# Two products with the state in a chunked delta-rule kernel: matmuls issued with the two batches alternating

## The reference, cut to what matters

```python
def step(Sst, inp):
    qt, kt, vt, gt, bt = inp
    Sst = Sst * jnp.exp(gt)[..., :, None]
    err = vt - jnp.einsum('bhk,bhkv->bhv', kt, Sst)
    Sst = Sst + bt[..., None, None] * kt[..., :, None] * err[..., None, :]
    ot = jnp.einsum('bhk,bhkv->bhv', qt, Sst)
    return (Sst, ot)
```

## Time and profile before

| | us |
|---|---|
| median of three runs | 1710.4 |
| lowest, highest | 1701.67, 1733.17 |
| profiled execution, first to last instruction | 1705.8 |
| PE busy, DVE busy in it | 1461.6, 1112.7 |
| mean granted TensorE clock in it | 0.919 of full |

### The profile page before, as it was taken

The page is one execution under the profiler, slowest core; times in us unless marked ns, Lnnn a source line. Parts: engine busy times, 40 slices in busy tenths (PEclk is TensorE's granted clock), DMA queues, the critical chain, the costliest instruction groups (busy, mean ns, idle before and its releaser), DMA issues.

```text
span 1705.8 us, 25673 instructions
## 1 busy us (share of the span) xinstructions
PE 1461.6 (86%) x9434; PEld 1185.9 (70%) x9434; DVE 1112.7 (65%) x2013; ACT 560.4 (33%) x1082; POOL 392.1 (23%) x351
## 2 busy tenths in 40 slices
PE   5786899999878699999978699999978599999977
PEld 4432788888733588888833488888853378888866
DVE  4399576667469567667549756766729856666742
ACT  1286222222268322122148422212228522222221
POOL 5034022212124112112124211221214311211210
PEclk8798899899999799899989799989989789999986
DMA  4000100000000010000000010000000000000001
GB/s 107 1 0 1 50 1 1 0 0 0 1 14 1 3 48 1 0 0 0 1 14 1 0 50 1 0 0 0 0 15 0 1 1 1 1 0 0 0 1 25
DMA packets 12493, 14.59 MB, mean 9 GB/s; under 512 B 3124, under 2 KB 8310, under 8 KB 12406
## 3 DMA queue, kind: packets, MB, share of 16 engines
q1 hardware_dynamic: 12406, 13.48, 2.7%
HBM read 12.43 MB, written 1.05 MB: 8 GB/s over the span
## 4 chain that ended last, share of the span: by engine, by line
PE 52%; DVE 25%; issue 19%; ACT 2%; POOL 1%; SPq 1%; DVEq 1%; POOLq 0%; DMA 0%; ACTq 0%
PE bank L653 9%; PE bank L707 8%; PE bank L703 8%; PE bank L690 5%; DVE qkv L950 4%; DVE ks L983 4%; PE bank L821 4%; DVE kq L981 3%; DVE tot L984 2%; PE bank L667 2%; PE bank L723 2%; PE bank L659 2%; PE bank L714 2%; DVE nmat L989 2%; DVE aq L990 2%
## 5 line engine op out<-in xcount | busy, mean ns | idle before, releaser
L653 PE MATMUL bank<-kq,ks 128*128 128x128 f32 x1536 | 231.6, 296 | 53.1 <-DVE tot L984 47.2
L981 DVE TENSOR_TENSOR kq<-kq,tot 128x512 f32<-128x512 f32 x160 | 138.4, 865 | 194.5 <-PE bank L653 191.4
L653 PEld LDWEIGHTS bank<-kq,ks 128*128 128x128 f32 x1536 | 200.9, 202 | 69.2 <-DVE tot L984 59.9
L629 PE MATMUL bank<-hT,gw 128*128 128x512 f32 x384 | 185.7, 621 | 38.1 <-DVE region L957 19.1
L950 DVE SCALAR_TENSOR_TENSOR qkv<-region,gchan,qkv 128x512 f32<-128x512 f32 x192 | 201.1, 1099 | 0.0
L371 POOL TENSOR_TENSOR qkv<-qkv,kq 128x509 f32<-128x509 f32 (+2 forms) x96 | 133.2, 1388 | 282.9 <-ACT qkv L454 277.9
L690 PE MATMUL bank<-region,nmat 128*128 128x64 f32 x1280 | 173.4, 280 | 2.3
L707 PE MATMUL bank<-tt,fmat 128*128 128x64 f32 x1280 | 170.6, 277 | 5.5 <-DVE fmat L1019 5.5
L629 PEld LDWEIGHTS bank<-hT,gw 128*128 128x128 f32 x384 | 73.6, 198 | 142.7 <-issue 103.7
L690 PEld LDWEIGHTS bank<-region,nmat 128*128 128x128 f32 x1280 | 163.6, 199 | 12.4 <-DVE nmat L989 7.5
L707 PEld LDWEIGHTS bank<-tt,fmat 128*128 128x128 f32 x1280 | 160.6, 195 | 7.5 <-DVE fmat L1019 6.0
(11 more groups left out here) (156 smaller groups left out, 2419.6 us busy)
## 6 DMA issues: line engine op xcount, KB each, us to landing
gw<-in_L_attn_Wq SPq DMA_DIRECT2D x4, 512.0 KB, 4.0
gw<-in_L_attn_Wk SPq DMA_DIRECT2D x4, 512.0 KB, 5.0
gw<-in_L_attn_Wv SPq DMA_DIRECT2D x4, 512.0 KB, 6.0
gwo<-in_L_attn_Wo SPq DMA_DIRECT2D x4, 512.0 KB, 4.9
x<-in_L_attn_hidden_states SPq DMA_DIRECT2D x2, 512.0 KB, 6.1
gfb<-in_L_attn_Wfb SPq DMA_DIRECT2D x4, 256.0 KB, 6.2
ggb<-in_L_attn_Wgb SPq DMA_DIRECT2D x4, 256.0 KB, 7.3
out<-x SPq DMA_DIRECT2D x2, 512.0 KB, 5.5
```

The source lines that it names most:

```text
L629: last = eng.matmul(bank[t][:, :], gw[:, t, kt, cols], hT[:, kt, toks], start=(kt == 0), stop=(kt == KT - 1))
L653: last = eng.matmul(o[:, :, u, :].rearrange("p a (n t) -> p a n t", t=h), unit(ks[:, p], u), half(kq[:, p, :, u * P:(u + 1) * P], h, 1), s ...
L981: eng.tensor_tensor(half(kq[:, p], h, 1), half(kq[:, p], h, 1), lower.rearrange("p (a n o) -> p a n o", a=1, o=1).broadcast_to((P, 2, nb, ...
```

## The change

Both pairs of loops are turned inside out. Each matmul, its operands, its output and its flags are what they were; only their order within the 8 is another: head 0 of batch 0, head 0 of batch 1, head 1 of batch 0, and so on. The wait ahead of the 8 stays ahead of them and the signal behind them stays with the last.

```diff
                     eng.wait_ge(state_ready, B * m + g + 1)
-                    for b in range(B):
-                        for u in range(G):
+                    for u in range(G):
+                        for b in range(B):
                             last = eng.matmul(unit(bank[4], u)[b * C:(b + 1) * C, :],
                                               kq[:, q, 0, u * P + b * C:u * P + (b + 1) * C],
                                               unit(state[:, b], u), start=True, stop=True)
...
-                    for b in range(B):
-                        for u in range(G):
+                    for u in range(G):
+                        for b in range(B):
                             eng.matmul(unit(bank[5], u)[b * C:(b + 1) * C, :],
                                        kq[:, q, 1, u * P + b * C:u * P + (b + 1) * C],
                                        unit(state[:, b], u), start=(u == 0), stop=False, skip_group_check=True)
```

## The result

The changed kernel takes 1811.97 us (median of 4 runs, 1805.08 to 1818.16), the old one 1709.87 (1701.67 to 1733.17). The ratio is 1.0616, 95% interval 1.0576 to 1.0656: 6% slower. Not one run of either kernel lies in the other's spread. Medians here are of all runs; ratios leave out runs over 1.5% above their kernel's fastest.

What follows compares the result with a forecast made beforehand. TensorE was 52% of the chain, VectorE 25%, with VectorE setting the pace in middle slots. First scan slots -1.2 and last slots -2.0 gave -3.2 us on the 1705.8 span: 1702.6, a median of 1707 us, range 1692 to 1727.

Steps and rivals of the forecast that it cites:

- what the order does to a product: Either product at full clock: alternating batches overlap throughout, so it takes 1.145 us instead of 1.58, 0.435 us less.
- The sum over L730: Sign in the profile after: L730's PE busy time falls from 55.8 to about 40 us.
- the middle slots: First product in 24 middle slots: gain 0, because VectorE sets the pace; L653 and L1031 start as before.
- the last slots: Last slot of each of 4 groups, both products: -0.5 us each, -2.0 us, as L753 comes 1.97 us after the start.
- the first scan slot: First product in 4 first scan slots, at 1.2 GHz: -0.3 us each, between 0 and 0.33, -1.2 us in all.
- 0 for the second product in the 28 slots: Second product in middle and first scan slots: gain 0, since PE then waits for VectorE's decays of level 1.
- the clock falls more often: Rival: thinner work behind the second product drops TensorE's clock; one more slow slot per group, +16.4 us, 1727; chance 0.13.
- a gap of 1.7 into one of 2.1: Behind the second product, ahead of level 2's product: the gain only lengthens PE's gap, in us.
- that the halves do not overlap: Rival: a product takes as long as before or 2.0 us, +3.6 us in all, 1710 to 1714; chance 0.06.

Runs made afterwards that it cites:

- e6: Changed kernel (both products alternating) plus 2 extra half-width matmuls behind the second product, both in the same output half: 1716.88 us, ratio 1.0052.
- e1: Old kernel with only the first product (L730) alternating, the second in its old order: 1709.22 us, ratio 1.0048.
- e4: Changed kernel plus 6 extra matmuls streaming 1 column each, in the gap behind the second product: 1806.34 us, ratio 1.059.
- e7: Changed kernel plus 2 extra half-width matmuls behind the second product, one in each output half, running at once: 1810.85 us, ratio 1.0566.
- e9: Old kernel, old orders, no filler; L667 streams 128 columns of ones instead of 1, L659 uses 128 rows instead of 16: 1694.85 us, ratio 0.9927.

## Why the prediction was wrong

The prediction chose next to no change, 1707 us, with a range of 1692 to 1727. Measured 1812.

**Right: what the order does to a product.** Forecast 1.145 us, measured 1.09 at full clock: the second half starts with the first, not 0.055 us behind it. The sum over L730 was forecast at 40 us and is 36.7; three of the four products in first scan slots ran partly at full clock (1.31 to 1.44 us, not 2.03).

**Right: the middle slots.** L653 and L1031 start where they did, and the gap grew by 0.49 (forecast 0.4). That alternation gives and costs nothing there at full clock is shown by e6 (34.26 us).

**Right: the last slots.** 2.50 became 1.97, as the sum of 1.97 had it, 2.1 us for the four. It is lost in the rest.

**Wrong in size: the first scan slot.** The term was -0.3 for each; e1 shows 0, the lower end of its bound. Not only the stretched tail of L984 but L981 as well ran into POOL's L343.

**The step that failed: 0 for the second product in the 28 slots, with the clock left to a rival, "the clock falls more often".** The rival's place was right, the gap behind the second product; its size was taken as "one more such slot in each group", 16.4 us net, and its chance as 0.13. In fact 19 of the 24 middle slots have that fall instead of 4, all 24 have some fall instead of 8, and together they take 80.4 us more. The first scan slots, which the rival left out, take 29.1 more. The old slots of 34.26 us have the same gap and keep their clock, and I read that as "it hangs on something that the change may tip" and then priced a small tip.

The price had a misreading too. The fall of the earlier trace rows stands in the slot from 318.10, which took 35.47 us, 1.2 more than 34.26. The slot of 39.20 in the earlier trace rows, from which the 4.9 us were taken, has its falls 23.3 and 30.2 us in, at other places. That 16 more slots at 4.9 us come to 78, near the 80.4, is luck.

Beyond that, two things were missed.

First, I counted what the change takes from this place as idle time, "a gap of 1.7 into one of 2.1". But e4 shows that idle time does not decide it here, and e6 and e7 that streaming in two halves at once did less for the clock than the same streaming in a row. Before, only the middle of a product had the two batches side by side. After, all of it does. The forecast named exactly this as the gain: "two batches share the array without taking time from one another". It is the loss as well.

Second, the falls are not independent. A slot with a fall is longer, so the next slot meets the clock's changes at another place. In the old kernel this leads back to slots without a fall: 16 of 24 have none. In the new one not one of the 24 is free of a fall. That is counted; that the place behind the second product catches the slots that used to get through is my reading of it, and the rule by which the chip decides was not measured.

**Rightly held unlikely: that the halves do not overlap (0.06).** The rule of the Trainium skill, "TensorE: Matmul & The Clock Gate", section "The mechanism" of Part 3, that weight loads overlap matmuls only when row groups differ, would have meant this, and it is contradicted again: 16 instructions with all rows and different output columns start in pairs. The Trainium skill's "TensorEngine Tiling (Array Packing)", section "Key Properties", says that different tiles can load weights and multiply in parallel. The trace agrees with that: two begin within 0.04 us.

What stays open is the rule behind the clock. The counts say only which of these kernels kept it and which did not.

## What to carry to other kernels

Before shortening TensorE work that nobody waits for, ask what it does for the clock: here a saving of 0.49 us in a place with slack brought slots of up to 43.6 us instead of 34.3 to 34.5. Packing two small products into the array at once shortens them truly, but in a stretch in which TensorE has little to stream it can cost more than it gives, and the busy time of the stretch does not show it; compare the granted clock slot by slot. In a kernel of many equal slots curing one thin place can move the fall to the next, so look at all slots after a change, and try the cheapest thickening first (more columns or rows in an instruction that is there anyway, as in e9).

## What the runs showed of the hardware

- Two matmul streams with the same rows and different halves of the output columns start within 0.04 us of one another, and each keeps its own pace of 0.11 us. In the old order, where the second batch begins while the first runs, they alternate at 0.054 (in rows of the last slot).
- 12 instructions that stream 1 column, busy for 1.50 us in the profile, left the falls of the clock as they were (22 of 24 slots); 12 that stream 128, busy for 1.60 us, removed them (0 of 24).
- The same 4 instructions behind the second product left the clock's falls at 5 of 24 slots when one followed the other (e6) and at 21 of 24 when two and two ran at once (e7).
- The product with 16 rows takes a little longer than with 128. In the old kernel, from its start to the next product's start:

```profile
270.13 1.15 PE L659 MATMUL bank<-beta,gsel 16*128 x8
...
271.21 1.10 PE L703 MATMUL bank<-fmat,tt 128*128 128x64 f32 x8
```

that is 1.08 us. With 128 rows (zeros in 112) in e9:

```profile
305.68 1.11 PE L661 MATMUL bank<-beta,gsel 128*128 x8
...
306.62 1.00 PE L705 MATMUL bank<-fmat,tt 128*128 128x64 f32 x8
```

0.94 us, at clock 1.00 like the other, and the slot is 0.35 us shorter with this and L667's edit together (34.26 to 33.91). How the rest divides was not tried.
